# Attention's float32 products on TensorE: the turns of values, maxima and rows and the logits' products issued beside numerators and denominators

## The reference

```python
xt = jnp.transpose(x, (0, 2, 1))
q = xt @ Wq.T
qh = q.reshape(B, T, NH, dk).transpose(0, 2, 1, 3)
scores = scale * jnp.einsum('bhqd,bhkd->bhqk', qh, qh)
logits = (scores * cmask + (1.0 - cmask) * NEG) * rmask
attn = jax.nn.softmax(logits, axis=-1)
ctx = jnp.einsum('bhqk,bhkd->bhqd', attn, qh)
out = ctx.transpose(0, 2, 1, 3).reshape(B, T, D) @ Wo.T      # transposed back
# then: expert logits from out, softmax, top 2 of 8 experts,
# h = silu(g) * u in each, weighted sum, plus a shared part times a sigmoid gate, plus x
```

## Time and profile before

| | us |
|---|---|
| median of 3 runs | 2041.2 (2037.2 to 2042.45) |
| profiled execution | 2043.55 |
| its span | 2041.7 |

### The profile page before, as it was taken

How to read it: one execution, slowest core, us unless ns; L and a number is a source line. 1 busy time by engine, 2 the same in 40 slices (tenths; PEclk the granted TensorE clock), 3 DMA queues, 4 the chain that set the end, 5 groups by cost and what they waited for, 6 DMA issues and landing times. The chain is left out here.

```text
span 2041.7 us, 28543 instructions
## 1 busy us (share of the span) xinstructions
PE 1917.3 (94%) x10324; PEld 1413.6 (69%) x10325; DVE 1022.2 (50%) x1661; ACT 705.0 (35%) x1276; POOL 657.9 (32%) x476
## 2 busy tenths in 40 slices
PE   4999999999999769899999999889999999999995
PEld 2444444444444357799999999878888888888874
DVE  3777777777777259343444443243433324242434
ACT  1566666666666522232233332231010101010000
POOL 3577776677765526111111111100101001010101
PEclk9999999999999879899999999989999999999998
DMA  6786667667663062432333322252302112130204
GB/s 124 111 132 103 106 126 110 108 101 131 104 98 60 19 235 91 148 125 82 109 120 125 111 80 78 90 163 73 103 22 82 42 60 66 37 102 1 93 17 154
DMA packets 117886, 196.17 MB, mean 96 GB/s; under 512 B 11280, under 2 KB 43024, under 8 KB 117808
## 3 DMA queue, kind: packets, MB, share of 16 engines
q1 hardware_dynamic: 106768, 158.98, 34.7%
q0 software_dynamic: 11040, 36.18, 6.1%
HBM read 100.71 MB, written 43.25 MB: 71 GB/s over the span
## 5 line engine op out<-in xcount | busy, mean ns | idle before, releaser
L382 DVE TENSOR_REDUCE maxcol<-ps_m 128x1 f32<-128x512 f32 x512 | 342.4, 683 | 180.8 <-PE ps_m L525 172.6
L321 ACT ACTIVATE e<-ps_e 128x512 f32<-128x512 f32 x512 | 297.4, 597 | 190.9 <-PE ps_e L520 189.5
L1289 POOL DMA_INDIRECT s_chosen<-routed,s_slot_now x64 | 61.5, 961 | 619.5 <-DVE s_total L1393 608.2
L126 POOL TENSOR_TENSOR e<-e 128x2048 f32<-128x2048 f32 x64 | 224.9, 3515 | 98.8 <-ACT e L321 98.8
L1347 DVE TENSOR_TENSOR s_h_f<-s_silu,s_ps_u 128x512 f32<-128x512 f32 x77 | 53.0, 688 | 394.3 <-PE s_ps_u L1419 344.6
L520 PE MATMUL ps_e<-qside,kside 98*128 98x512 f32 x512 | 242.0, 475 | 8.8 <-ACT e L321 7.8
L520 PEld LDWEIGHTS ps_e<-qside,kside 98*128 98x128 f32 x512 | 96.5, 189 | 212.7 <-ACT e L321 175.5
L525 PE MATMUL ps_m<-kside,qside 97*128 97x512 f32 x512 | 216.4, 428 | 16.4 <-DMA qside<-row_mask 13.5
L1315 ACT ACTIVATE s_silu<-s_ps_g 128x512 f32<-128x512 f32 x77 | 46.0, 598 | 531.3 <-PE s_ps_g L1419 531.3
L1016 DVE TENSOR_TENSOR e_h_f<-e_silu,e_ps_h 128x256 f32<-128x256 f32 (+1 forms) x108 | 45.1, 418 | 249.7 <-ACT e_silu L857 249.7
L1430 PE MATMUL s_ps_y<-s_d_hi,s_h_hi 128*128 128x512 f32 x352 | 139.6, 396 | 9.0 <-DVE s_h_lo L1367 9.0
(11 more groups left out here) (233 smaller groups left out, 4276.0 us busy)
## 6 DMA issues: line engine op xcount, KB each, us to landing
routed<-e_y SPq DMA_DIRECT2D x36, 512.0 KB, 2.8
kside<-q_hi SPq DMA_DIRECT2D x64, 256.0 KB
qside<-qm_hi SPq DMA_DIRECT2D x64, 256.0 KB
x_f<-in_x SPq DMA_DIRECT2D x16, 512.0 KB, 3.8
kside<-q_lo SPq DMA_DIRECT2D x32, 256.0 KB
qside<-qm_lo SPq DMA_DIRECT2D x32, 256.0 KB
attn<-xo SPq DMA_DIRECT2D x32, 256.0 KB, 3.7
keep_rows<-attn SPq DMA_DIRECT2D x8, 1024.0 KB, 5.6
```

The costliest lines, as they stand in the source:

```text
L126: eng.tensor_tensor(into, into, e[k + 1][:, heads, :], ALU.add).then_inc(done, 1)
L321: act.activation(e[kb][:, g, :], ps_e[g % 2][:, :], ACT.Exp, scale=SCALE).then_inc(e_done, 1)
L382: dve.reduce_max(maxcol[par][:, g * KB + kb:g * KB + kb + 1], ps_m[g % 2][:, :], AX.X).then_inc(max_done, 1)
L1289: pool.indirect_dma_start(out=chosen[k][s % 2][:], out_offset=None, in_=routed, in_offset=bass.IndirectOffsetOnAxis(ap=slot_now[:, k, s:s ...
```

## The change

On TensorE, `turn_maxima` and `turn_values` are issued directly ahead of the numerators at kb = 0 and g = 1; the two halves of `turn_rows` directly behind the numerators at kb = 1 and 2; `partial_logits` directly behind those at kb = 3; `logits` behind the denominators at kb = 3, g = 3. On ScalarE, `copy_maxima` moves from behind the exponential of (0,3) to behind that of (0,1), and `context_high` from behind (0,2) to behind `copy_maxima` there. No operation is added or removed. Where a step of an even unit had twelve separate float32 groups and an odd one eight, both now have six.

```diff
--- before.py
+++ after.py
@@ -334,10 +334,10 @@
                 for g in range(HG):
                     if known(i, n):
                         weights(i, n, kb, g)
-                    if (kb, g) == (0, 2) and known(i, n, -2):
+                    if (kb, g) == (0, 1) and known(i, n, 1):
+                        copy_maxima(i, n)
+                    if (kb, g) == (0, 1) and known(i, n, -2):
                         context_high(i, n)
-                    if (kb, g) == (0, 3) and known(i, n, 1):
-                        copy_maxima(i, n)
                     if (kb, g) == (1, 1) and known(i, n, 3):
                         copy_values(i, n)
                     if kb in (1, 2) and g == 3 and even and known(i, n, -4, hi=NU):
@@ -498,6 +498,20 @@
             parts(ps_o[:, :], (lambda t: wo_hi[:, t, c], lambda t: wo_lo[:, t, c]),
                   (lambda t: c_hi[s + t][:, :], lambda t: c_lo[s + t][:, :]), KT).then_inc(o_mm, 1)
 
+        def fp32_group(i, n, kb, before):
+
+            if kb == 0 and known(i, n, 1):
+                turn_maxima(i, n)
+            if kb == 0 and known(i, n, 3):
+                turn_values(i, n)
+            if before:
+                numerators(*before)
+            if n % 2 == 0 and known(i, n, -4, hi=NU):
+                if kb in (1, 2):
+                    turn_rows(i, n, kb - 1)
+                if kb == 3:
+                    partial_logits(i, n)
+
         def step(i, n):
             u = RING * i + n
             if isinstance(i, int) and u == 0:
@@ -523,26 +537,19 @@
                         tile = (KB * (u + 2) + kb) * HG + g
                         upto(pe, max_done, tile - 1)
                         nc.tensor.matmul(ps_m[g % 2][:, :], qside[s2][0:MAXROW, g, cols], kside[s2][0:MAXROW, g, :], start=True, stop=True).then_inc(m_mm, 1)
-                    if g == 0 and kb == 0 and known(i, n, 3):
-                        turn_values(i, n)
                     if g == 0 and kb == 2 and known(i, n, 4):
                         project(i, n)
-                    if g == 1 and before:
-                        numerators(*before)
-                    if g == 2 and kb == 0 and known(i, n, 1):
-                        turn_maxima(i, n)
-                    if g == 2 and kb in (1, 2) and n % 2 == 0 and known(i, n, -4, hi=NU):
-                        turn_rows(i, n, kb - 1)
-                    if g == 0 and kb == 3 and n % 2 == 0 and known(i, n, -4, hi=NU):
-                        partial_logits(i, n)
-                    if g == 2 and kb == 3 and n % 2 == 0 and known(i, n, -4, hi=NU):
-                        logits(i, n)
+                    if g == 1:
+                        fp32_group(i, n, kb, before)
                     if g == 2 and kb >= 2 and n % 2 == 1 and known(i, n, -3, hi=NU):
                         out_rows(i, n, kb - 2)
                     if g == 3 and kb == 1 and known(i, n, -1):
                         denominators(u - 1, 1)
-                    if g == 3 and kb == 3 and known(i, n):
-                        denominators(u, 0)
+                    if g == 3 and kb == 3:
+                        if known(i, n):
+                            denominators(u, 0)
+                        if n % 2 == 0 and known(i, n, -4, hi=NU):
+                            logits(i, n)
 
         run_units(step, -4, 5)
```

## The result

| | before | changed |
|---|---|---|
| median, us (6 runs each) | 2041.74 | 2033.09 |
| range, us | 2037.2 to 2043.78 | 2031.91 to 2035.29 |
| profiled execution, us | 2043.55 | 2035.29 |

Changed over before is 0.9963, with a 95% interval of 0.9950 to 0.9976: some 8 us faster.

The account below looks back on a forecast made before the run. Attention was taken to end when TensorE's queue ends, with late starts the cost. Gains 6.1 + 0 + 2.1 + 2.8 = 11.0, taken as 10.5, gave 2033.05 profiled and 2030.7 us median; range 2020 to 2038.

Parts of the forecast that it names:

- High half (0.32) and maxima (0.11): At kb 0: moving the high half gains 0.32 us a unit, maxima's turn costs 0.11; 6.1 us in all.
- Values and maxima ahead of numerators (0): Values' turns at kb 0 cost 0.44 in either place, switch taken as 0.21: no gain, ends -3 and +4 us.
- the last part: List of signs to look for in the trace, among them about 0.75 us from M(0,1) to numerators.
- the list of starts: Expected kb 0 starts relative to M(0,0): M(0,1) 0.46, numerators 1.45, E(0,2) 2.44, its exponential ready 2.98 us.
- Rows and logits behind strips (0.15 a unit): Rows behind numerators twice, logits behind denominators once: 0.05 us saved each, 14 even units, 2.1 us.
- Partial logits (0.20): Partial logits behind numerators at kb 3: E(2,2) to E(3,2) shortens by 0.20 us in 14 units, 2.8 us.
- 0.54 + 0.35 on offer: At partial logits: 0.54 us wait for ScalarE's copy plus 0.35 strip switch, of which only 0.20 was forecast.
- the forecast's slower rival: High half waiting for c_f delays the exponential of (0,2) and TensorE; 1.1 us later costs 5 us; 5%.
- the slack: Time the high half has to spare before the exponential of (0,2) is ready, put at 0.6 us.
- the tail at 0: Start and tail of attention, chains of DMA and copies that keep their order, were forecast to change by 0.
- The rival of a switch on every float32 group: Each of 128 removed separate float32 groups saves 0.10 us, 12.8 us more than forecast, giving 2018; 10%.

Follow-up runs that it names:

- the first kernel above: Only the high half's copy moved behind the exponential of (0,1), on the kernel before: 2033.12 us, 0.9962 of before.
- the experiment on q: On the changed kernel, ScalarE copies q_hi right behind q_f at (2,1), not behind the exponential of (2,2): 2026.65 us, 0.9923 of before.
- the late product: On the changed kernel, one more 128 x 512 product on GpSimd ahead of c_f, into a tile nobody reads: 2048.26 us in one run.

## Why the prediction was right

It said 2030.7 us, 2020 to 2038, faster; the median is 2033.09. By its steps:

*High half (0.32) and maxima (0.11).* Both as forecast. E(0,2) to E(1,1) fell from 2.2 to 1.86, and the first kernel above gives the same 3.55 that unit 1 had shown. In unit 12 of the changed kernel E(0,2) to E(1,2) is 3.95 (299.56, 303.51), since the rows now stand in between with 0.41. This is also where the gain is: alone it is the whole of the change's effect.

*Values and maxima ahead of numerators (0).* M(0,1) to numerators is 0.87 (297.69, 298.56): a step of 0.23, five turns less one by their starts 0.43, and 0.21 for the switch, the value taken between 0.11 and 0.33. The 0.75 that the last part named, and the 0.99 in the list of starts, disagree with the item's own sum, 0.88, which is what came.

*Rows and logits behind strips (0.15 a unit).* Half right. E(2,2) comes 0.42 behind where numerators alone would put it (309.13 to 309.55) and E to E is 0.54, so a group of rows costs 0.38. The logits cost 0.44 by the same reading: from the denominators in front to the M behind 1.78 us pass (314.93, 316.71), where 1.34 would without them. Alone they had cost 0.45 (M to M 0.91 before, 318.33 to 319.24, less two steps). Two of three groups gained, 0.1 a unit.

*Partial logits (0.20).* 4.24, where 4.25 was named, and the wait at E(3,1) where it was expected; the experiment on q shows its cause. The rest of the 0.54 + 0.35 on offer was not had, for the reason in the forecast: taking a filler away uncovers what it hid.

*Counted for units that don't have it.* In units 2 and 30 the high half waited for c_f, and the gain of 0.21 there became nothing or a loss. GpSimd, VectorE, ScalarE and TensorE of the changed kernel in unit 30, in this order:

```profile
651.39 2.13 POOL L208 TENSOR_TENSOR c_f<-num,den 128x512 f32<-128x512 f32 x1 [7.07 <-DVE den L389]
```

and

```profile
651.23 1.16 DVE L126 TENSOR_TENSOR e<-e 128x1024 f32<-128x1024 f32 x1
```

and

```profile
653.55 0.63 ACT L259 ACTIVATE c_hi<-c_f 128x512 fp32r<-128x512 f32 x1 [1.08 <-POOL c_f L208]
```

and

```profile
654.72 0.99 PE L534 MATMUL ps_e<-qside,kside 98*128 98x512 f32 x2 [1.57 <-ACT e L321]
```

The high half waited 1.08 us and TensorE stood still for 1.57. The product was as long in this unit before (2.13 at 661.65), but there the high half stood further back and hardly waited (663.81). The mechanism is the forecast's slower rival, and its point was near: the slack, 0.6 in the forecast, is 0.5, because the list of starts has numerators and what follows them 0.11 too late (its 2.44 for E(0,2) came as 2.33). It decides in 2 units of 30, and pushed on by the late product in all of them it makes the kernel slower than before.

So the steps come to 0.48 us in an even unit and 0.23 in an odd one, where 0.56 and 0.21 were forecast: 9.6 us between units 3 and 30 in place of 10.2. Unit 2 gained nothing (18.40 in both kernels), and unit 30 is 17.38 long in place of 15.91. Not all of this is the high half: moved alone it makes the unit 16.38 long, and the groups alone make it 15.31, so the two together lose more than their sum, and what else waits there was not taken apart.

*Some luck in the sum.* The last logits come 10.9 us earlier, and the forecast for attention was 11.0. Two things that it had not counted make up for unit 30. E(0,0) of unit 0 happened to start 0.7 earlier (63.74 in place of 64.42; the kernels here lie between 63.3 and 64.5). And from the start of unit 31 to the last logits it is 40.8 us in place of 42.9; the high half alone gives the same 40.8, so this, too, belongs to its place, though the prediction had only 0.21 there and the tail at 0.

*The rival of a switch on every float32 group* is out: 128 groups fewer without the high half moved gave at most 3 us, and a kernel with 64 groups more is 12 us faster. What a group in strips pays (0.35) belongs to the change between whole-array and strip products: beside numerators, partial logits bring only their own columns, 0.88 + 0.55 from numerators to E (312.36, 313.24, 313.79) against 0.99 without them. The Trainium skill, "TensorEngine Tiling (Array Packing)", Key Properties, says that a change of tiling mode drains TensorE. The traces agree as to where a price is paid; whether it is a drain or a weight load that nothing hides, no run here separates. Turns of float32 between ordinary products, which change the type but not the mode, pay nothing (294.90 and 295.49 above).

## What to carry to other kernels

With two banks between an engine that makes tiles and one that reads them, a tile's start is held by everything in the reader's queue: here a copy that nobody was in a hurry for belonged where TensorE had long work of another kind, not between two exponentials. Work without a switch price is best put where the maker would wait, and not gathered: 0.55 us of turns cost 0.09 in such a place. A part that is taken out of a run may have been hiding a wait, so the time of the run without it is read from a unit of the same trace that lacks it, not from its length.

## What had not been expected of the hardware

GpSimd's product of 128 x 512, 1.29 us in unit 12, took 2.13 in unit 30 (651.39 above), beside an addition of 128 x 1024 on VectorE that began 0.16 us earlier. The same stood in the trace of before, 2.13 at 661.65 beside an addition at 661.49. In the kernel with the late product it is the added product that starts 0.16 behind the addition and takes 2.13 (663.03), and c_f right behind it takes 1.26. So the length goes with the addition and not with the unit; no run takes the addition away to show that it is the cause. It is what makes the high half late in unit 30. And kernels with equal instructions behind attention still differ there, from 1322.7 to 1326.5 us in one execution each, so a change of a few us is read from the starts of a stage and not from one time.
